# Two subtractions of an attention pipeline, on GpSimd instead of VectorE

## The chip, the cores and the metric

One core of a Trainium2 chip runs the whole kernel in one launch. The metric is the device time of that launch in microseconds. TensorE does the matrix products, VectorE and ScalarE the work on what TensorE leaves in PSUM, GpSimd reads and writes SBUF alone, and SyncE issues most DMAs.

## What is computed

A decoder block over x (8 sequences of 256 tokens, width 512): self attention, cross attention to a context of 256 tokens of width 128, and a mixture of 32 experts. Cut to what matters here:

```python
# self attention of layernorm(x): 16 heads of 32, 4 key heads
cw = sigmoid(sum(abs(x), -1, keepdims=True))
q = dot(x * cw, Wq);  k, v = split(dot(x, Wkv), 2, -1)
qk = einsum('bhid,bhjd->bhij', q, k) * scale + alibi
qk = where(allowed, -1e9, qk);  attn = softmax(qk);  x1 = x + dot(attn @ v, Wo) + bo
# cross attention of layernorm(x1): 32 heads of 16, 8 key heads, k = v = ctx
scores = einsum('bkgsd,bktd->bkgst', qh, kh) / scale
x2 = x1 + softmax(scores) @ vh
# 32 experts, 4 for each token, capacity 128, and a shared one
out = x2 + moe(layernorm(x2)) + shared(layernorm(x2))
```

## The kernel before

The program is one block for each engine, written out in order by hand; engines meet at semaphores. The attention part is a pipeline: `pipelined` calls each engine's body for k = 0 to 9, which the text calls step k. In step k the self attention of sequence k (flag a, k = 0 to 7), the cross attention of sequence k - 1 (flag x, k = 1 to 8) and the routing of sequence k - 2 (flag g, k = 2 to 9) are interleaved. The expert part comes behind and is not touched.

Softmax takes its row maxima ahead of the exponentials. TensorE makes 32 units of cross scores (L1143, two matmuls each, into two halves of qx in turn), and VectorE takes each unit's maximum (L868); TensorE may write unit v only when maximum v - 2 is done. Between these units stand other things, at unit numbers fixed by constants such as `AT_QUERY`, `AT_CONTEXT` and `AT_SELF`: the projection of the queries (L1088), the transposes of values and context (L1097, L1104), of the third norm (L1025), the logits of the router (L1073), and from unit 23 the self scores (L1116, L1118), whose maxima are L859. Then TensorE transposes the maxima (L1168, L1186), and the second half of the step does the scores again with the exponentials and the weighting.

Scores are made exactly enough by splitting. The queries qf (128 x 768, f32, L839 on VectorE) are rounded by ScalarE to qh, and the remainder ql = qf - qh is what L845 computes on VectorE, right behind the maximum of unit 4 (AT_QUERY[3] + 3). It signals q_split. SyncE waits for that and copies qh, qh and ql into the rows of qs by three DMAs of 384 KB; the self scores wait for qs_in. The context keys (128 x 256) are split in three: kp[0] by ScalarE from PSUM, the remainder kr by VectorE (L849), kp[1] by ScalarE, and kp[2] = kr - kp[1] by VectorE (L853), which signals c_split. SyncE then copies them into kxs, which the next step uses. Behind the queries' DMAs SyncE has, in this order: the third norm to xnd, the sequence to out, the wait for c_split and the six DMAs into kxs, then the shift rows of the maxima.

GpSimd's part of step k is: add the bias bo to the two tiles of the sequence (L467), then the powers and products of the norms (L435, L441) as their statistics come, and with flag g the list of slots (L482) and eight indirect DMAs that scatter into slot_table (L487). The last norm of step k and its scatters end during the first units of step k + 1, so in steps 3 to 7 the bias additions stand behind eight scatters. The lines of the order and the signals:

```python
                    hold(sp, s["q_split"], k + 1)
                    for m, part in enumerate((qh, qh, ql)):
                        go(qs[m:SPLIT_ROWS:3].bitcast(F32), part.bitcast(F32), "qs_in")
```

In step 0 there are no cross units, and VectorE does L839, L845, L849 and L853 in a row.

Of the kernel before, what the change touches and what calls it, by code (L numbers as in the profile page):

```python
# [6 lines left out]
F32 = mybir.dt.float32  # L7
# [3 lines left out]
ALU = mybir.AluOpType  # L11
# [97 lines left out]
def build(nc, x, ctx, wq, wkv, wo, bo, gw, gb, w1, w2, w3, sg, su, sd,  # L109
# [15 lines left out]
    with st:  # L125
# [54 lines left out]
        qf = place(DC * SQ).rearrange("p (c n) -> p c n", c=DC)  # L180
        qh = place(DC * SQ, dt=F32R).rearrange("p (c n) -> p c n", c=DC)
        ql = place(DC * SQ, dt=F32R).rearrange("p (c n) -> p c n", c=DC)
# [4 lines left out]
        kr = place(S)  # L187
        kp = [place(S // 2, dt=BF16) for _ in range(3)]
# [82 lines left out]
        s = {n: sem(n) for n in names}  # L271
# [38 lines left out]
        AT_QUERY = (-1, -1, -1, 1)  # L310
# [119 lines left out]
        @block.gpsimd  # L430
        def _(pool):
            def norm_scale(n, count):

                pool.wait_ge(s[f"ln{n}_stats"], count)
                nc.gpsimd.tensor_tensor(stats[n][2][:], stats[n][1][:, :, 1], power[:], ALU.pow  # L435
                                        ).then_inc(s[f"ln{n}_rstd"], 1)

            def norm_shift(n, count):

                hold(pool, s[f"ln{n}_rstd"], count)  # L440
                nc.gpsimd.tensor_tensor(shift[n][:], shift[n][:], stats[n][2][:], ALU.mult  # L441
                                        ).then_inc(s[f"ln{n}_shift"], 1)

            nc.gpsimd.memset(ones[:], 1.0)
            nc.gpsimd.memset(onesb[:], 1.0)
            nc.gpsimd.memset(seen[:], 0.0)
            nc.gpsimd.memset(vx, 1.0)

            nc.gpsimd.memset(arena[:, attention_top:ARENA], 0.0).then_inc(s["clear"], 1)
            for n, (place_, value) in enumerate(((qxs[96:P], 0.0), (kxs[0][96:P], 0.0), (kxs[0][96:98], 1.0),  # L450
                                                 (kxs[1][96:P], 0.0), (kxs[1][96:98], 1.0))):
                pool.wait_ge(s["clear"], n + 1)
                nc.gpsimd.memset(place_, value).then_inc(s["clear"], 1)
            pool.wait_ge(s["clear"], 6)
            pool.wait_ge(s["const_moved"], 1)
            nc.gpsimd.memset(power[:], -0.5).then_inc(s["const_ready"], 1)
            pool.wait_ge(s["const_ready"], 1)
            norm_scale(1, 1)
            norm_shift(1, 1)

            @pipelined(pool)
            def _(k, a, x, g, n):
                if a:

                    pool.wait_ge(s["xn1"], k + 1)
                    for t in range(2):
                        op = nc.gpsimd.tensor_tensor(tile(k, t), tile(k, t), bo_s[:], ALU.add)  # L467
                    op.then_inc(s["bo_added"], 1)
                if n:
                    norm_scale(1, k + 2)  # L470
                    norm_shift(1, k + 2)
                if a:
                    norm_scale(2, k + 1)
                if x:
                    norm_scale(3, k)
                    norm_shift(3, k)
                if g:

                    pool.wait_ge(s["slot_ready"], k - 1)
                    if isinstance(k, int) and k == 2:  # L480
                        pool.wait_ge(s["init_out"], 16)
                    nc.gpsimd.tensor_copy(sdat[:, :, 0].rearrange("p (t k) -> p t k", t=2),  # L482
                                          token[:, bass.ds(k * 2 - 4, 2)].unsqueeze(2).broadcast_to([P, 2, TOPK])
                                          ).then_inc(s["sdat_ready"], 1)
                    hold(pool, s["sdat_ready"], k - 1)
                    for c in range(2 * TOPK):
                        nc.gpsimd.indirect_dma_start(  # L487
                            slot_table, bass.IndirectOffsetOnAxis(ap=slot_u[:, c:c + 1], axis=0), sdat[:, c, :], None,
                            bounds_check=NE * CAP - 1, oob_is_err=False).then_inc(s["sc_out"], 16)

            pool.wait_ge(s["sc_out"], B * 2 * TOPK * 16)
            pool.wait_ge(s["xnd_out"], B * 16)

            pool.wait_ge(s["ks_in"], B * 96)
            pool.wait_ge(s["x2"], B * 3)
            pool.wait_ge(s["slot_ready"], B)
            pool.dma_start(iw[:].rearrange("p (e c) -> p e c", c=2), slot_table.rearrange("(e p) c -> p e c", p=CAP)
                           ).then_inc(s["iw_in"], 16)
            pool.wait_ge(s["iw_in"], 16)

            ids = iw[:].rearrange("p (e c) -> p e c", c=2)

            def fetch(e):

                if e >= FETCH:
                    pool.wait_ge(s["xe_t"], e - FETCH + 1)
                nc.gpsimd.indirect_dma_start(
                    fetched[e % FETCH], None, xnd, bass.IndirectOffsetOnAxis(ap=ids[:, e, 0:1], axis=0),
                    bounds_check=N - 1, oob_is_err=False).then_inc(fetch_in[e % FETCH], 16)

            def add_base(n):

                pool.wait_ge(s["res_final"], n * 4 + 4)
                pool.dma_start(out.rearrange("b (u p) d -> p (b u) d", p=P)[:, n * 4:n * 4 + 4],
                               res[:, n * 4 * D:n * 4 * D + 4 * D].rearrange("p (t d) -> p t d", t=4),
                               accum_op=ALU.add).then_inc(y_out, 16)

            for e in range(FETCH):
                fetch(e)
            pool.wait_ge(s["x2_out"], B * 16)  # L520
            flat = out.rearrange("b s d -> (b s) d")
            for e in range(NE):
                if FETCH <= e + FETCH - 1 < NE and e > 0:
                    fetch(e + FETCH - 1)
                pool.wait_ge(s["y_ready"], e + 1)
                if e > 0:
                    pool.wait_ge(y_out, adds_before(e) * 16)
                nc.gpsimd.indirect_dma_start(  # L528
                    flat, bass.IndirectOffsetOnAxis(ap=ids[:, e, 0:1], axis=0), ye[e % 2], None,
                    bounds_check=N - 1, oob_is_err=False, compute_op=ALU.add).then_inc(y_out, 16)  # L530
                if base_after(e) is not None:
                    pool.wait_ge(y_out, adds_before(e) * 16 + 16)
                    add_base(base_after(e))
            pool.wait_ge(y_out, adds_before(NE) * 16)
# [176 lines left out]
        def _(dve):  # L711
# [116 lines left out]
            def _(k, a, x, g, n):  # L828
# [11 lines left out]
                                     cwb[:, GLOB:S].unsqueeze(1).broadcast_to([P, DC, SQ]), ALU.mult  # L840
                                     ).then_inc(s["q_scaled"], 1)

                def queries_low():
                    dve.wait_ge(s["q_hi"], k + 1)
                    v_.tensor_tensor(ql, qf, qh.bitcast(F32), ALU.subtract).then_inc(s["q_split"], 1)  # L845

                def context_rem():
                    dve.wait_ge(s["c_hi"], k + 1)
                    v_.tensor_tensor(kr, va[:, 0:S], kp[0], ALU.subtract).then_inc(s["c_rem"], 1)  # L849

                def context_low():
                    dve.wait_ge(s["c_mid"], k + 1)
                    v_.tensor_tensor(kp[2], kr, kp[1], ALU.subtract).then_inc(s["c_split"], 1)  # L853

                def self_max(u):

# [5 lines left out]
                if x:  # L862

                    for v in range(XU):
                        kv, t, half = v // 4, v // 2 % 2, v % 2
                        dve.wait_ge(s["xs_unit"], k * XU - XU + v + 1)
                        col = t * XH + query_at(kv * 4 + half * 2)
                        v_.reduce_max(mxx[:, col:col + 3:2], xbank[v % 2].rearrange("p (h n) -> p h n", h=2), AX.X  # L868
                                      ).then_inc(s["x_max"], 1)
                        if a:  # L870
                            if v == AT_QUERY[3] + 1:
                                queries()
                            elif v == AT_QUERY[3] + 3:
                                queries_low()
                            elif v == AT_CONTEXT + 3:
                                context_rem()
                            elif v == AT_CONTEXT + 6:
                                context_low()
                            if v in AT_SELF:
                                self_max(AT_SELF.index(v))  # L880
                    if not a:
# [6 lines left out]
                else:  # L888
                    if a:
                        queries()  # L890
                        queries_low()
                        context_rem()
                        context_low()
                if a:
                    for u in range(len(AT_SELF) if x else 0, AU):
                        self_max(u)
# [542 lines left out]
```

## Time and profile before

| what | value |
|---|---|
| median of 3 runs | 1155.16 us (1154.0 to 1156.06) |
| the profiled execution | 1159.79 us |
| its span | 1158.0 us |
| busy: TensorE, VectorE, ScalarE, GpSimd | 1004.4, 583.8, 332.2, 214.3 us |
| mean granted clock of TensorE | 0.877 |
| steps 1 to 7 | some 82 to 88 us each, between 102 and 707 us |

The profile is one execution. Busy times are shares of different stages, so they don't tell by themselves what ends last; the chain of waits does, since it is followed back from the last instruction. The granted clock is TensorE's, 1.00 for 2.4 GHz and 0.50 for 1.2 GHz. A DMA's time to landing runs from its issue to its signal.

### The profile page before, as it was taken

The numbers are of one execution on the slowest core, as the hardware profiler recorded it, in microseconds if no ns is written. First come the engines' busy times: TensorE is split into PE (matmuls) and PEld (weight loads), VectorE is DVE, ScalarE is ACT, GpSimd is POOL, SyncE is SP. The second block draws the span as 40 slices with busy tenths as digits, with TensorE's granted clock in tenths as the row PEclk, the third lists the DMA queues.
The fourth block names the chain that finished last, engine by engine and source line by source line (L and its number), as shares of the span: only waits on it lengthen the run. The fifth ranks groups of instructions, "written<-read, shape, count | busy, mean of one in ns | idle before, by whom it ended". The sixth has DMA issues, their size and how long they took to land.

```text
span 1158.0 us, 15121 instructions
## 1 busy us (share of the span) xinstructions
PE 1004.4 (87%) x5745; PEld 532.4 (46%) x5784; DVE 583.8 (50%) x1296; ACT 332.2 (29%) x639; POOL 214.3 (19%) x212
## 2 busy tenths in 40 slices
PE   2666898998998998998999798897999999999983
PEld 1535445545545545545535444233444444444441
DVE  1335836857857857857866947723122222222221
ACT  3021064154154154154164143161111111111110
POOL 6001001002102102102102203004322232322222
PEclk9678589689689689689589999698999999999997
DMA  6402202302302302302302404008277776777782
GB/s 214 133 2 73 56 2 74 92 2 74 92 3 74 92 3 73 92 3 73 92 3 74 129 2 128 2 1 291 47 182 211 210 208 215 221 185 218 209 231 33
DMA packets 95579, 119.26 MB, mean 103 GB/s; under 512 B 11185, under 2 KB 72049, under 8 KB 95504
## 3 DMA queue, kind: packets, MB, share of 16 engines
q1 hardware_dynamic: 80644, 96.52, 26.7%
q0 software_dynamic: 11408, 18.64, 8.2%
q10 hardware_dynamic: 3456, 3.15, 0.9%
q8 instruction: 46, 0.75, 0.3%
q14 instruction: 25, 0.20, 0.1%
HBM read 70.90 MB, written 21.07 MB: 79 GB/s over the span
## 4 chain that ended last, share of the span: by engine, by line
PE 71%; DVE 14%; DMA 4%; ACT 4%; issue 3%; POOL 2%; SPq 0%; ACTq 0%; POOLq 0%; DVEq 0%
PE qa L1393 9%; PE qx L1143 5%; PE qa L1257 5%; PE pt L1362 5%; DVE mxx L868 5%; PE qx L1381 4%; PE vb L1210 4%; ACT arena L540 4%; PE qa L1088 4%; PE vb L1037 4%; PE qx L1037 4%; PE qx L1199 3%; PE qa L1118 3%; PE qa L1037 3%; PE va L1057 3%
## 5 line engine op out<-in xcount | busy, mean ns | idle before, releaser
L540 ACT ACTIVATE arena<-qx 128x512 f32<-128x512 f32 x268 | 151.2, 597 | 309.7 <-PE qx L1199 187.4
L868 DVE TENSOR_REDUCE mxx<-qx 128x2 f32<-128x512 f32 x256 | 166.3, 684 | 45.1 <-PE qx L1143 42.8
L1143 PE MATMUL qx<-arena 96*128 96x256 bf16 x512 | 120.6, 344 | 31.4 <-DVE mxx L868 30.9
L435 POOL TENSOR_TENSOR rstd<-mv,power 128x2 f32<-128x2 f32 x24 | 16.9, 702 | 651.6 <-DVE mv L732 651.6
L540 ACT ACTIVATE arena<-qa 128x512 f32<-128x512 f32 (+2 forms) x116 | 63.9, 553 | 217.3 <-PE qa L1393 95.6
L1393 PE MATMUL qa<-arena 128*128 128x512 f32 x256 | 115.2, 593 | 0.8 <-ACT arena L540 0.8
L1199 PE MATMUL qx<-arena 98*128 98x512 bf16 x256 | 98.9, 428 | 8.4 <-ACT arena L540 5.6
L528 POOL DMA_INDIRECT out<-arena,iw x32 | 50.4, 1576 | 209.4 <-DVE arena L997 137.0
L1210 PE MATMUL vb<-arena 128*32 128x256 f32 x1024 | 87.6, 416 | 1.8 <-ACT arena L540 1.1
L1143 PEld LDWEIGHTS qx<-arena 96*128 96x128 bf16 x512 | 41.5, 113 | 91.7 <-DVE mxx L868 74.6
L1118 PE MATMUL qa<-ks,qs 100*128 100x128 f32 x256 | 76.3, 451 | 7.7 <-DMA qs<-arena 7.7
L916 DVE RECIPROCAL rd<-va 128x192 f32<-128x192 f32 x32 | 43.4, 1358 | 58.1 <-PE va L1252 58.1
L487 POOL DMA_INDIRECT slot_table<-sdat,slot_u x64 | 65.8, 1028 | 23.5 <-issue 17.1
L1118 PEld LDWEIGHTS qa<-ks,qs 100*128 100x128 f32 x256 | 65.2, 312 | 7.5
L1393 PEld LDWEIGHTS qa<-arena 128*128 128x128 f32 x256 | 46.5, 192 | 46.9 <-issue 46.9
L1257 PE MATMUL qa<-arena 128*128 128x512 f32 x128 | 60.6, 619 | 5.9 <-DVE arena L918 5.9
L1381 PE MATMUL qx<-arena 128*128 128x512 f32 x128 | 62.0, 608 | 2.3 <-DVE arena L997 2.3
L1362 PE MATMUL pt<-arena 128*128 128x512 f32 x128 | 59.5, 609 | 4.8 <-DVE res L989 2.6
L1006 DVE SCALAR_TENSOR_TENSOR arena<-arena,qa 128x256 f32<-128x256 f32 x32 | 13.5, 421 | 91.8 <-ACT arena L540 91.8
L1199 PEld LDWEIGHTS qx<-arena 98*128 98x128 bf16 x256 | 24.0, 101 | 76.8 <-ACT arena L540 45.9
L859 DVE TENSOR_REDUCE mx<-qa 128x4 f32<-128x512 f32 x64 | 44.0, 689 | 23.1 <-PE qa L1118 22.2
L540 ACT ACTIVATE arena<-arena 128x512 f32<-128x512 f32 (+3 forms) x40 | 25.5, 637 | 84.6 <-DVE arena L839 53.1
(172 smaller groups left out, 1425.6 us busy)
## 6 DMA issues: line engine op xcount, KB each, us to landing
arena<-in_L_ffn_w SPq DMA_DIRECT2D x96, 512.0 KB, 6.0
qs<-arena SPq DMA_DIRECT2D x24, 384.0 KB, 5.0
arena<-arena SPq DMA_DIRECT2D x72, 128.0 KB, 2.4
res<-in_x SPq DMA_DIRECT2D x8, 512.0 KB, 9.0
xnd<-arena SPq DMA_DIRECT2D x8, 512.0 KB, 7.0
out<-res SPq DMA_DIRECT2D x8, 512.0 KB, 7.3
out<-res POOLq DMA_DIRECT2D x4, 1024.0 KB, 9.3
ks<-arena SPq DMA_DIRECT2D x48, 64.0 KB, 1.9
```

The source lines that it names most:

```text
L487: nc.gpsimd.indirect_dma_start(slot_table, bass.IndirectOffsetOnAxis(ap=slot_u[:, c:c + 1], axis=0), sdat[:, c, :], None, bounds_check=NE ...
L540: nc.scalar.activation(dst, src, func, **kw).then_inc(s[signal], 1)
L868: v_.reduce_max(mxx[:, col:col + 3:2], xbank[v % 2].rearrange("p (h n) -> p h n", h=2), AX.X).then_inc(s["x_max"], 1)
L1037: op = mm(bank, w[:, c, m * P:m * P + P], xt3[:, bass.ds(n * 2, 2), c, :], start=c == 0, stop=c == DC - 1)
L1118: op = mm(abank[u % 2][:, h * P:h * P + P], qs[0:rows, q * 4 + h, blk * GLOB:blk * GLOB + P], ks[0:rows, blk, q, :], start=False, stop=h == 3)
L1143: op = mm(xbank[v % 2][:, h * S:h * S + S], qxs[0:XSPLIT_ROWS, query_at(kv * 4 + half * 2 + h), t * P:t * P + P], kxs[1 - k % 2][0:XSPLIT_ ...
L1199: mm(xbank[v % 2], kxs[1 - k % 2][0:XSPLIT_ROWS + SHIFT_ROWS, kv, t * P:t * P + P], qxs[0:XSPLIT_ROWS + SHIFT_ROWS, h:h + 3:2, :], start=T ...
L1210: op = mm(vb[at_:at_ + 32, kv % 2 * S:kv % 2 * S + S], vx[:, t, kv, :], ex[(2 * w + g4 // 2) % 4][:, g4 % 2 * S:g4 % 2 * S + S], start=t = ...
L1257: op = mm(qa[:, t * D:t * D + D], at[:, q, t * P:t * P + P], wo_s[:, q, :], start=q == 0, stop=q == DC - 1)
L1362: op = mm(pt[:, D:2 * D], ht_sh[:, c, m * P:m * P + P], sd_s[:, c, :], start=c == 0, stop=c == DC - 1)
L1381: op = mm(xbank[0], hte[e % 2][:, c, :], h2[e % EU][:, c, :], start=c == 0, stop=c == 1)
L1393: op = mm(abank[e % 2], xgt[e % 2][:, c, :], h13[e % EU][:, c, :], start=c == 0, stop=c == DC - 1)
```

## The change

The subtractions L845 and L853 are taken out of VectorE's order and put into GpSimd's, behind the bias additions of the same step and ahead of the norms. Each waits there for the same signal of ScalarE (q_hi, c_mid) and gives the same signal (q_split, c_split). Operands, sizes and everything else stay.

```diff
@@ gpsimd, step k
                     for t in range(2):
                         op = nc.gpsimd.tensor_tensor(tile(k, t), tile(k, t), bo_s[:], ALU.add)
                     op.then_inc(s["bo_added"], 1)
+                    pool.wait_ge(s["q_hi"], k + 1)
+                    nc.gpsimd.tensor_tensor(ql, qf, qh.bitcast(F32), ALU.subtract).then_inc(s["q_split"], 1)
+                    pool.wait_ge(s["c_mid"], k + 1)
+                    nc.gpsimd.tensor_tensor(kp[2], kr, kp[1], ALU.subtract).then_inc(s["c_split"], 1)
                 if n:
@@ vector, step k
-                def queries_low():
-                    dve.wait_ge(s["q_hi"], k + 1)
-                    v_.tensor_tensor(ql, qf, qh.bitcast(F32), ALU.subtract).then_inc(s["q_split"], 1)
-
...
-                def context_low():
-                    dve.wait_ge(s["c_mid"], k + 1)
-                    v_.tensor_tensor(kp[2], kr, kp[1], ALU.subtract).then_inc(s["c_split"], 1)
...
                             if v == AT_QUERY[3] + 1:
                                 queries()
-                            elif v == AT_QUERY[3] + 3:
-                                queries_low()
                             elif v == AT_CONTEXT + 3:
                                 context_rem()
-                            elif v == AT_CONTEXT + 6:
-                                context_low()
```

GpSimd around the end of one of the steps 2 to 5 and the start of the next, before (the slot list, the scatters of the old step, then the bias additions and norms of the new one):

```order
L482 COPY sdat<-token 128x8
L487 DMA slot_table<-sdat,slot_u 4096x2 x8
L467 TENSOR_TENSOR res<-res,bo_s 128x512 x2
L435 TENSOR_TENSOR rstd<-mv,power 128x2
L441 TENSOR_TENSOR shift<-shift,rstd 128x2
L435 TENSOR_TENSOR rstd<-mv,power 128x2 x2
```

The same place after:

```order
L486 COPY sdat<-token 128x8
L491 DMA slot_table<-sdat,slot_u 4096x2 x8
L467 TENSOR_TENSOR res<-res,bo_s 128x512 x2
L470 TENSOR_TENSOR arena<-arena 128x768
L472 TENSOR_TENSOR arena<-arena 128x256
L435 TENSOR_TENSOR rstd<-mv,power 128x2
L441 TENSOR_TENSOR shift<-shift,rstd 128x2
```

The 768 and 256 columns (ql and kp[2]) now stand behind eight scatters and two additions. VectorE from the start of a middle step to the first self maximum (L859), before; mxx are the cross maxima, mx the self maxima:

```order
L834 TENSOR_TENSOR arena<-va,arena 128x256
L868 TENSOR_REDUCE mxx<-qx 128x2 x3
L839 TENSOR_TENSOR arena<-qa,arena 128x768
L868 TENSOR_REDUCE mxx<-qx 128x2 x2
L845 TENSOR_TENSOR arena<-arena 128x768
L868 TENSOR_REDUCE mxx<-qx 128x2 x6
L849 TENSOR_TENSOR arena<-va,arena 128x256
L868 TENSOR_REDUCE mxx<-qx 128x2 x3
L853 TENSOR_TENSOR arena<-arena 128x256
L868 TENSOR_REDUCE mxx<-qx 128x2 x10
L859 TENSOR_REDUCE mx<-qa 128x4
```

And after, where L864 are the cross maxima, L843 the queries, L849 the remainder kr and L855 the self maxima:

```order
L838 TENSOR_TENSOR arena<-va,arena 128x256
L864 TENSOR_REDUCE mxx<-qx 128x2 x3
L843 TENSOR_TENSOR arena<-qa,arena 128x768
L864 TENSOR_REDUCE mxx<-qx 128x2 x8
L849 TENSOR_TENSOR arena<-va,arena 128x256
L864 TENSOR_REDUCE mxx<-qx 128x2 x13
L855 TENSOR_REDUCE mx<-qa 128x4
```

Two instructions are gone from between the maxima; the rest keeps its order.

## Rows read from the trace of the kernel before

**Rows 1.** The page, part 4: shares of the chain by engine.
```profile
PE 71%; DVE 14%; DMA 4%; ACT 4%; issue 3%; POOL 2%; SPq 0%; ACTq 0%; POOLq 0%; DVEq 0%
```

**Rows 2.** VectorE's groups by form: count, busy us, mean ns, idle before.
```profile
L845 DVE TENSOR_TENSOR arena<-arena 128x768 fp32r<-128x768 f32 x8 | 7.7, 957 | 0.9 <-ACT arena L540 0.9
...
L853 DVE TENSOR_TENSOR arena<-arena 128x256 bf16<-128x256 f32 x8 | 3.3, 416 | 0.5 <-ACT arena L540 0.5
```

**Rows 3.** The chain in step 0: start us, us, what.
```profile
38.06 0.97 DVE arena L845
...
46.60 1.30 PE qa L1118 x4
```

**Rows 4.** The chain in step 1.
```profile
115.58 0.87 DVE arena L845
...
122.55 0.33 DVE arena L853
```

**Rows 5.** The chain in step 2, at the context transposes.
```profile
203.41 0.36 PE va L1104 x2
```

**Rows 6.** ScalarE's timeline in step 2, the copy of the values: start us, us.
```profile
202.50 0.47 ACT L540 ACTIVATE arena<-va 128x384 f32<-128x384 f32 x1
```

**Rows 7.** GpSimd's timeline in steps 3 to 7: scatters and bias additions.
```profile
287.84 1.48 POOL L487 DMA_INDIRECT slot_table<-sdat,slot_u  x1 [0.31 <-issue]
...
291.89 2.50 POOL L467 TENSOR_TENSOR res<-res,bo_s 128x512 f32<-128x512 f32 x2
...
375.14 0.97 POOL L487 DMA_INDIRECT slot_table<-sdat,slot_u  x1 [0.30 <-issue]
...
378.68 2.50 POOL L467 TENSOR_TENSOR res<-res,bo_s 128x512 f32<-128x512 f32 x2
...
461.52 1.74 POOL L487 DMA_INDIRECT slot_table<-sdat,slot_u  x1 [0.30 <-issue]
...
465.83 2.51 POOL L467 TENSOR_TENSOR res<-res,bo_s 128x512 f32<-128x512 f32 x2
...
553.59 2.50 POOL L467 TENSOR_TENSOR res<-res,bo_s 128x512 f32<-128x512 f32 x2
...
641.23 2.50 POOL L467 TENSOR_TENSOR res<-res,bo_s 128x512 f32<-128x512 f32 x2
```

**Rows 8.** VectorE's timeline in steps 4 and 5.
```profile
375.12 1.02 DVE L845 TENSOR_TENSOR arena<-arena 128x768 fp32r<-128x768 f32 x1
...
461.47 0.95 DVE L845 TENSOR_TENSOR arena<-arena 128x768 fp32r<-128x768 f32 x1
```

**Rows 9.** The three DMAs into qs of step 5.
```profile
DMA to landing us min/median/max: 3.7/5.1/6.1
```

**Rows 10.** TensorE's timeline, steps 3 to 7: first self scores, transpose of cross maxima.
```profile
302.24 1.20 PE L1118 MATMUL qa<-ks,qs 100*128 100x128 f32 x4
...
390.08 0.75 PE L1118 MATMUL qa<-ks,qs 100*128 100x128 f32 x4
...
476.17 1.07 PE L1118 MATMUL qa<-ks,qs 100*128 100x128 f32 x4
...
486.45 0.63 PE L1168 MATMUL vb<-ident,mxx 128*32 128x128 f32 x2
...
565.85 1.31 PE L1118 MATMUL qa<-ks,qs 100*128 100x128 f32 x4
...
651.12 0.75 PE L1118 MATMUL qa<-ks,qs 100*128 100x128 f32 x4
...
659.82 0.40 PE L1168 MATMUL vb<-ident,mxx 128*32 128x128 f32 x2 [1.01 <-DVE mxx L868]
```

**Rows 11.** Stretches: busy us (count) of five engines, granted clock, DMA share, GB/s.
```profile
460.00:463.00 3.00, 1.05 (x7) 0.26 (x5) 3.00 (x6) 2.61 (x4) 2.45 (x2) 0.96 0.02 1
...
477.00:487.00 10.00, 10.00 (x47) 8.45 (x46) 8.59 (x15) 0.00 (x0) 0.00 (x0) 0.50 0.00 0
...
652.00:660.00 8.00, 6.01 (x42) 4.38 (x42) 8.00 (x14) 0.00 (x0) 0.00 (x0) 1.00 0.00 0
```

More of the change, by code:

```diff
@@ L890, in _ @@
                         queries()
-                        queries_low()
                         context_rem()
-                        context_low()
                 if a:
```

## The prediction

> **What bounds the kernel now.** I read the page's chain of waits first: TensorE holds 71% of it and VectorE 14%, so an instruction taken from VectorE pays only where VectorE is the chain [rows 1]. The edit lies in the attention pipeline, steps k = 0 to 7, so next I read the chain inside single steps. Step 0 has no cross maxima to hide anything: the remainder of the queries (L845, from 38.06 us, 0.97 us long) releases three DMAs into qs, and TensorE's first self score L1118 starts at 46.60, held by them [rows 3]. The reader should see one fixed delay there, from the end of the remainder to that matmul: 46.60 - 39.03 = 7.57 us. In steps 1 to 7 VectorE interleaves the cross maxima with the four small operations, and L845 is on the chain in all seven, as in step 1 with 0.87 us [rows 4]. The low part of the context keys (L853) is on it in step 1 alone, for 0.33 us [rows 4]; later TensorE's transposes and logits end last around it.
>
> Then I read GpSimd's timeline, since it gets the work. In steps 3 to 7 it is late: it still issues the eight scatters of the step before, and ends its two bias additions only at 294.39, 381.18, 468.34, 556.09 and 643.73 us [rows 7]. VectorE's L845 of steps 4 and 5 begins at 375.12 and 461.47 [rows 8], 6 to 7 us before that.
>
> **What leaves VectorE.** Eight L845 of 0.957 us and eight L853 of 0.416 us [rows 2]. In step 1 both are on the chain: 0.87 + 0.33 = 1.20 us gained [rows 4]. In step 2, without L845 TensorE would reach the context transposes (L1104) some 0.87 us before 203.41 [rows 5], but they wait for ScalarE's copy of the values, which ends at 202.50 + 0.47 = 202.97 [rows 6] and does not hang on L845. So 203.41 - 203.01 = 0.40 us is gained, and L853 gives nothing. Steps 3 to 7 have the same sequence, so 0.4 us is what each could gain if nothing else comes late.
>
> **What GpSimd pays.** The trace has no GpSimd subtraction of 768 columns. The nearest row is its two-input addition of 512 columns, a pair of which takes 2.50 us [rows 7], 1.25 each; 768 / 512 x 1.25 = 1.88 us, which I take. Bounds: VectorE's own 0.95 us [rows 2] below, and two passes, 3.76 us, above, since the output is fp32r, which no GpSimd row here has. The 256-column operation is 0.63 us by the same row; behind it stand only norm_scale and norm_shift, which wait for statistics that VectorE makes only in the softmax stage, so it costs nothing. What SyncE has queued behind q_split and c_split (xnd, out, kxs) moves back by up to 8 us and is read a step later; it is covered as long as the six issues for kxs are through before the shift rows are wanted at the end of the maxima.
>
> The Trainium skill (GPSIMD Engine Reference, 3.1) gives GpSimd about 2.6 cycles per element for such an operation, by which I estimate 768 x 2.6 / 1.2 GHz = 1.66 us; the sum below would then be about 1.1 us smaller.
>
> **The scatters get faster.** In step 5 one scatter takes 1.74 us and not 0.97; it starts at 461.52, with VectorE's L845 (461.47 to 462.42) [rows 7, 8]. Steps 6 and 7 show 1.75 at the same place, step 3 shows 1.48, and step 4 shows 0.97 although L845 begins 0.02 us before that scatter [rows 7, 8]. With L845 gone from VectorE I take these away: GpSimd is done 0.51 us earlier in step 3, 0.77 in step 5, 0.78 in steps 6 and 7. The Trainium skill (SBUF: State Buffer, "SBUF: two separate sides") says that a VectorE operation with two SBUF inputs and GpSimd exclude each other from a shared port pair; three of the five steps agree fully, step 4 does not. By that page the maxima, which read PSUM, stay free of the new GpSimd work too.
>
> **Where the queries land now.** The three DMAs behave alike in every step, those of step 5 with 3.7, 5.1 and 6.1 us from issue to landing [rows 9]. So the self scores can start at the end of the bias additions, less the scatter's gain, plus 1.88 + 7.57 = 9.45 us. Against the first L1118 of now, which is held by the maxima [rows 10]:
> step 3: 293.88 + 9.45 = 303.33 against 302.24, +1.09;
> step 4: 381.18 + 9.45 = 390.63 against 390.08, +0.55;
> step 5: 467.57 + 9.45 = 477.02 against 476.17, +0.85;
> step 6: 555.31 + 9.45 = 564.76 against 565.85, hidden, so the 0.40 of VectorE is gained;
> step 7: 642.95 + 9.45 = 652.40 against 651.12, +1.28.
> Together +3.37 us. What VectorE saves ahead of that point in steps 3, 4, 5 and 7 is not gained: TensorE only waits longer. GpSimd's own start does not move against the step, as it hangs on the third norm of the step before. Step 0: GpSimd has done its additions long before, the remainder takes 1.88 for 0.95, all of it on the chain, +0.93. Steps 1 and 2: GpSimd has issued no scatters and is free before the queries are ready; the data has slack (by step 5's rows 462.42 + 7.57 = 469.99 against a start at 476.17 [rows 8, 10]), so -1.20 and -0.40. Sum: 3.37 + 0.93 - 1.60 = +2.7 us.
>
> **The clock.** In the self scores of step 5 the granted clock was 0.50, in those of step 7 it was 1.00 [rows 11]; from the first L1118 to the transpose L1168 this was 486.45 - 476.17 = 10.28 us and 659.82 - 651.12 = 8.70 us [rows 10]. At 460 to 463 us TensorE was busy 1.05 of 3 us, and its clock began to fall within them, to a mean of 0.96 [rows 11]. In step 7 a wait of some 2 us is put just ahead of the self scores, where none was, so I let it lose the higher level (2.4 GHz) there: 10.28 - 8.70 = +1.58. Whether it does is about even, and any step can win or lose as much when its stalls move.
>
> **Forecast.** +2.7 + 1.58 = +4.3 us. The profiled execution took 1159.79 us with a span of 1158.0, 4.6 above the median of 1155.16; the sum is of differences inside that execution, and I add it to the median: 1159.5 us.
>
> **Rivals.**
> (A) Forecast, 1157.5 to 1162: chance 0.48.
> (B) Faster: the landing is hidden everywhere. Mechanism: the subtraction at VectorE's own 0.95 us, or scatters that shorten in step 4 as well, bring qs in before TensorE asks, so VectorE's saving counts. It decides once the data is there 1.5 to 2 us sooner than worked out (1.28 of step 7 plus the 0.4 saved). Price: -1.20 - 6 x 0.40 = -3.6, step 0 between 0 and +0.93, so about 1152.3. For it: four waits of only 0.6 to 1.3 us against the old start. Against it: the 0.95 bound alone does not do it in steps 3 and 7. Chance 0.09.
> (C) Nothing to measure: the step 7 clock stays, and the wait is half a microsecond shorter in steps 3 to 5 and 7: 2.7 - 2.0 = +0.7, about 1156. Chance 0.22.
> (D) The clock goes against more steps: two of steps 3 to 6 lose another 1.58 each by a later rise, 1162.7. Against: their self scores are already at 0.50 in large part. Chance 0.13.
> (E) GpSimd's fp32r output doubles the subtraction: 1.88 us more in steps 0, 3, 4, 5 and 7, and step 6 turns from -0.40 to +0.80: 9.4 + 1.2 = +10.6 more, 1170. No row speaks for it; on VectorE fp32r output costs 0.957 us, under three times the 0.416 of a third of the columns [rows 2]. Chance 0.08.
>
> A change that doesn't do what it says is left out: GpSimd's order shows the two operations behind the bias additions in every step.
>
> **Numbers.** The likeliest is (A), 1159.5. The range takes in (A), (C), (D) and the half of (B) that step 0 spoils, and leaves (E) out: 1153.5 to 1165. A measurement here can tell about 0.2%, 2.3 us. Slower by more, above 1157.5: (A) nearly whole, (D), (E), 0.66. Within: (C) and edges of (A) and (B), 0.25. Faster, below 1152.9: 0.09.
>
> **What would show it.** In the profile after: L470 of GpSimd near 1.9 us; it starts where the bias additions end in steps 3 to 7; no scatter of 1.75 us; idle time of TensorE ahead of L1118 put down to the DMA into qs in steps 3, 4, 5 and 7 (1 to 2.5 us each) and not in 1, 2 and 6; about 8.5 us of it in step 0; the clock at 0.50 in the self scores of step 7. Without those waits the forecast is wrong, and (B) or (C) holds; an L470 near 3.8 us means (E).

## The result, and the profile after

The changed kernel took 1162.79 us (median of 4 executions, 1162.59 to 1163.26), the kernel before 1155.05 us beside it: 7.7 us more, a ratio of 1.0068 with a 95% interval of 1.0050 to 1.0085. The forecast was 1159.5 us, 4.3 us more. The two profiled executions are only 1162.62 - 1159.79 = 2.8 us apart, because executions of the kernel before spread more than that (1151.4 to 1160.6 us on one chip in the next comparison), and its profiled one is at the slow end. So the profiles serve to compare places, and the ratios to compare kernels. The ratios leave out slow executions, more than 1.5% above the fastest of their kernel (one each of x8 and x11 below).

The page after, parts 1 and 4 (busy us by engine; shares of the chain), against [rows 1]:

```profile
PE 1010.0 (87%) x5784; PEld 539.2 (46%) x5784; DVE 575.4 (50%) x1280; ACT 332.0 (29%) x639; POOL 230.5 (20%) x228
...
PE 64%; DVE 12%; DMA 7%; POOL 6%; issue 6%; ACT 4%; SPq 1%; POOLq 0%; ACTq 0%; DVEq 0%
```

GpSimd's share of the chain went from 2% to 6% and that of DMAs from 4% to 7%. Where they entered is seen in step 3, whose chain (start us, us, what) now runs through GpSimd's queue:

```profile
289.44 0.97 POOL slot_table L491
290.42 0.30 issue
290.72 0.97 POOL slot_table L491
291.69 2.52 POOL res L467 x2
294.21 1.76 POOL arena L470
295.97 0.02 issue
295.99 0.55 SPq L334
...
297.23 6.07 DMA qs<-arena
303.30 0.14 issue
303.43 0.59 PE qa L1106
304.02 0.75 PE qa L1108 x4
```

Scatters, bias additions, subtraction, SyncE, the third DMA, then TensorE: no maximum is on this chain. The first self scores by step, from TensorE's timeline, answer to [rows 10]; the bracket is TensorE's idle time and what ended it:

```profile
303.43 0.59 PE L1106 MATMUL qa<-masks,identb 128*128 128x512 bf16 x1 [1.08 <-DMA qs<-arena]
...
391.53 0.58 PE L1106 MATMUL qa<-masks,identb 128*128 128x512 bf16 x1 [0.94 <-DMA qs<-arena]
...
477.98 0.38 PE L1106 MATMUL qa<-masks,identb 128*128 128x512 bf16 x1 [0.77 <-DMA qs<-arena]
...
565.17 0.53 PE L1106 MATMUL qa<-masks,identb 128*128 128x512 bf16 x1 [0.53 <-DMA qs<-arena]
...
654.22 0.63 PE L1106 MATMUL qa<-masks,identb 128*128 128x512 bf16 x1
```

Steps 3 to 6 wait for the queries, step 7 does not: of the signs that the prediction named, the waits came in steps 3, 4 and 5 (0.8 to 1.1 us), and in step 6 in place of step 7. Here GpSimd's groups by form, after (count, busy us, mean ns), for what VectorE did in [rows 2]:

```profile
L470 POOL TENSOR_TENSOR arena<-arena 128x768 fp32r<-128x768 f32 x8 | 14.5, 1808 | 43.0 <-ACT arena L544 43.0
L472 POOL TENSOR_TENSOR arena<-arena 128x256 bf16<-128x256 f32 x8 | 5.4, 669 | 8.0 <-ACT arena L544 8.0
```

### The profile page after: what moved, and what is told of

It is laid out like the page before. It is cut to its first block, busy times and chain, and to the rows that moved or that the text cites. A ratio compares the mean times of both kernels' runs of the same rounds, so it can differ in the third digit from the quotient of the medians.

```text
span 1160.8 us, 15160 instructions
## 1 busy us (share of the span) xinstructions
PE 1010.0 (87%) x5784; PEld 539.2 (46%) x5784; DVE 575.4 (50%) x1280; ACT 332.0 (29%) x639; POOL 230.5 (20%) x228
## 4 chain that ended last, share of the span: by engine, by line
PE 64%; DVE 12%; DMA 7%; POOL 6%; issue 6%; ACT 4%; SPq 1%; POOLq 0%; ACTq 0%; DVEq 0%
PE qa L1383 8%; PE qa L1247 5%; PE pt L1352 5%; PE qx L1133 4%; PE vb L1200 4%; PE qx L1371 4%; PE vb L1027 4%; PE qx L1027 4%; PE qx L1189 3%; ACT arena L544 3%; PE qa L1108 3%; PE qa L1027 3%; DMA qs<-arena 3%; DMA out<-arena,iw 2%; DVE mxx L864 2%
## 5 line engine op out<-in xcount | busy, mean ns | idle before, releaser
L864 DVE TENSOR_REDUCE mxx<-qx 128x2 f32<-128x512 f32 x256 | 165.6, 685 | 49.0 <-PE qx L1133 47.0
L1133 PEld LDWEIGHTS qx<-arena 96*128 96x128 bf16 x512 | 44.2, 116 | 81.1 <-DVE mxx L864 63.5
L1108 PE MATMUL qa<-ks,qs 100*128 100x128 f32 x256 | 80.6, 471 | 0.0
L1108 PEld LDWEIGHTS qa<-ks,qs 100*128 100x128 f32 x256 | 68.9, 328 | 8.2
L491 POOL DMA_INDIRECT slot_table<-sdat,slot_u x64 | 62.9, 982 | 23.5 <-issue 17.1
L1247 PE MATMUL qa<-arena 128*128 128x512 f32 x128 | 60.6, 619 | 5.9 <-DVE arena L908 5.9
L1352 PE MATMUL pt<-arena 128*128 128x512 f32 x128 | 57.8, 594 | 4.8 <-DVE res L979 2.6
L855 DVE TENSOR_REDUCE mx<-qa 128x4 f32<-128x512 f32 x64 | 44.3, 692 | 31.3 <-PE qa L1108 30.2
L1106 PE MATMUL qa<-masks,identb 128*128 128x512 bf16 x64 | 39.8, 622 | 11.9 <-DMA qs<-arena 11.9
```

What stands on the lines that cost most here:

```text
L491: nc.gpsimd.indirect_dma_start(slot_table, bass.IndirectOffsetOnAxis(ap=slot_u[:, c:c + 1], axis=0), sdat[:, c, :], None, bounds_check=NE ...
L1108: op = mm(abank[u % 2][:, h * P:h * P + P], qs[0:rows, q * 4 + h, blk * GLOB:blk * GLOB + P], ks[0:rows, blk, q, :], start=False, stop=h == 3)
L1133: op = mm(xbank[v % 2][:, h * S:h * S + S], qxs[0:XSPLIT_ROWS, query_at(kv * 4 + half * 2 + h), t * P:t * P + P], kxs[1 - k % 2][0:XSPLIT_ ...
L1247: op = mm(qa[:, t * D:t * D + D], at[:, q, t * P:t * P + P], wo_s[:, q, :], start=q == 0, stop=q == DC - 1)
L1352: op = mm(pt[:, D:2 * D], ht_sh[:, c, m * P:m * P + P], sd_s[:, c, :], start=c == 0, stop=c == DC - 1)
```

## The experiments

All numbers of steps are from the first key matmul of the step to the first self score, in the profiled execution of each kernel. The ratio is to executions of the kernel before on the same chip; chips and hours differ (its median was 1155.05, 1156.66, 1157.04 and 1161.54 us). It is not the quotient of the two medians, from which it differs by up to 0.2%. The columns of steps come from one execution each, and its time is not the median: x10's profiled one took 1155.37 us where its median is 1163.66, x9's 1161.54 for 1169.49.

| kernel | ratio [95%] | step 0 | steps 1, 2 | steps 3 to 7 | steps 0 to 7 | the rest of the span |
|---|---|---|---|---|---|---|
| before | 1 | 21.16 | 26.60, 26.98 | 26.90 27.15 26.88 28.81 26.44 | 210.9 | 947.1 |
| x1 before again | 0.9985 [0.9966, 1.0004] | 21.26 | 26.56, 27.34 | 26.89 28.80 26.44 26.89 27.11 | 211.3 | 946.7 |
| after | 1.0068 [1.0050, 1.0085] | 22.10 | 27.43, 26.59 | 27.79 27.88 27.47 27.47 28.38 | 215.1 | 945.7 |
| x5 after again | 1.0100 [1.0079, 1.0121] | 22.55 | 25.40, 26.62 | 27.75 27.92 27.48 28.38 29.25 | 215.4 | 949.9 |
| x2 delay only | 1.0089 [1.0059, 1.0119] | 23.18 | 28.28, 28.83 | 28.28 27.97 27.46 27.70 27.51 | 219.2 | 945.5 |
| x9 queries only | 1.0070 [1.0041, 1.0100] | 21.44 | 27.48, 26.54 | 27.75 28.02 27.48 27.48 27.52 | 213.7 | 946.0 |
| x10 keys only | 1.0017 [0.9992, 1.0042] | 21.01 | 26.34, 27.43 | 26.89 26.89 26.90 28.90 26.44 | 210.8 | 942.8 |
| x7 before, scatters late | 0.9993 [0.9979, 1.0008] | 21.69 | 28.56, 27.10 | 26.44 26.89 27.11 26.95 26.89 | 211.6 | 946.6 |
| x3 no subtraction | 0.9987 [0.9963, 1.0010] | 20.85 | 27.38, 26.54 | 26.54 28.37 29.23 26.08 26.66 | 211.7 | 943.6 |
| x11 between the additions | 0.9969 [0.9942, 0.9997] | 21.91 | 25.56, 26.54 | 26.64 26.54 26.72 28.41 28.39 | 210.7 | 943.0 |
| x6 ahead of the additions | 0.9927 [0.9903, 0.9951] | 21.88 | 25.95, 26.55 | 26.55 26.74 29.26 26.09 26.55 | 209.6 | 940.4 |
| x4 scatters late | 0.9917 [0.9889, 0.9945] | 21.99 | 27.41, 26.59 | 26.54 26.63 26.76 26.77 26.54 | 209.2 | 942.0 |
| x8 x4, step 0 on VectorE | 0.9946 [0.9926, 0.9967] | 20.49 | 27.48, 26.60 | 26.55 26.65 26.54 26.73 26.54 | 207.6 | 938.7 |
| x12 x6, step 0 on VectorE | 0.9914 [0.9882, 0.9946] | 20.49 | 26.04, 26.58 | 26.54 26.65 29.16 26.09 26.68 | 208.2 | 940.8 |

**x1, the kernel before again.** No edit.

> The kernel before, unchanged. The change cost 7.7 us between medians (1155.05 to 1162.79) but only 2.8 us between the two profiled executions (1159.79 to 1162.62), so the profiled execution of before was 4.7 us over its own median. If that was one odd execution, with the clock's levels falling elsewhere, this profile comes out near 1155 us and its steps 1 to 7 are shorter than those of the first one. If a profile always costs this kernel some 4.7 us, it is near 1159.8 again. The median should be 1155 us, ratio 1.000, either way.

1156.35 us (1151.43 to 1159.78), and again a profile of 1159.78 us. Whether a profiled execution of this kernel always costs more is left open by it: x7's (1159.98) was also the highest of its ten, x10's the lowest of its eleven. The equal total is chance in part: step 7 took 27.11 and not 26.44 us up to the self scores, step 4 28.80 and not 27.15. What differs is where the clock stands. Stretches of x1 in the self scores of steps 5 and 7 (us, busy by engine, then the granted clock), against [rows 11]:

```profile
478.00:486.00 8.00, 6.14 (x43) 4.33 (x42) 8.00 (x15) 0.00 (x0) 0.00 (x0) 1.00 0.01 2
649.00:657.00 8.00, 8.00 (x37) 6.78 (x37) 6.95 (x11) 0.00 (x0) 0.00 (x0) 0.50 0.00 0
```

In the first profile step 7 had the clock at 1.00 there and step 5 at 0.50; in x1 it is the other way round. So neither is a property of a step. In the profiles of before, x1, x3, x6, x7, x8, x10, x11 and x12, one or two steps of each had their self scores at 1.00 (8.70 us to L1168, where 0.50 takes 10.5); in those of the changed kernel (after, x5), x2 and x9, which have the late landing, and of x4, none had. That 1.8 us and the 2 us that a step now and then loses ahead of the self scores (28.4 to 29.3 in the table) wander from execution to execution.

**x2, the delay alone.** VectorE keeps both subtractions; GpSimd repeats the queries' one, and its signal counts.

```diff
-  v_.tensor_tensor(ql, qf, qh.bitcast(F32), ALU.subtract).then_inc(s["q_split"], 1)
+  v_.tensor_tensor(ql, qf, qh.bitcast(F32), ALU.subtract).then_inc(s["q_dve"], 1)
...
   op.then_inc(s["bo_added"], 1)
+  pool.wait_ge(s["q_dve"], k + 1)
+  nc.gpsimd.tensor_tensor(ql, qf, qh.bitcast(F32), ALU.subtract).then_inc(s["q_split"], 1)
```

> VectorE keeps both subtractions, as before; GpSimd does the subtraction of the queries once more behind the bias additions, and only its signal releases SyncE. So the late landing stands alone, without any relief of VectorE. Late landing as the cause: q_split in steps 3 to 7 as late as after the change plus up to 0.8 us for the lengthened scatter, waits of TensorE for qs of 0.5 to 2.5 us, step 0 later by 1.9 us; 1155 + 6 to 9, 1161 to 1165 us. Rival, that the change's loss lies in how the clock falls once VectorE has less to do: the landing costs only what the sum had, some 4 us, about 1159 us.

1167.67 us, ratio 1.0089: with the delay and no relief the whole loss is there; that it is more than the change's 1.0068 can't be told, since the intervals overlap. The waits of TensorE for qs, in x2 and then in the changed kernel (us in total, times, longest):

```profile
PE qa L1120 <- DMA qs<-arena: 12.7, 6, 9.6
```
```profile
PE qa L1106 <- DMA qs<-arena: 11.9, 5, 8.6
```

The longest is step 0, so x2 has 3.1 us in five steps and the changed kernel 3.3 in four. The delay is not quite alone in x2: in steps 0 and 3 the keys' subtraction, still on VectorE, meets GpSimd's and takes 0.93 and 1.20 us in place of 0.42. VectorE's row and GpSimd's in step 3:

```profile
300.04 1.20 DVE L855 TENSOR_TENSOR arena<-arena 128x256 bf16<-128x256 f32 x1
```
```profile
299.14 1.81 POOL L470 TENSOR_TENSOR arena<-arena 128x768 fp32r<-128x768 f32 x1
```

With the queries' subtraction still on VectorE too, GpSimd's timeline of x2 shows the long scatter of step 3 again:

```profile
292.62 1.49 POOL L489 DMA_INDIRECT slot_table<-sdat,slot_u  x1 [0.30 <-issue]
294.41 0.97 POOL L489 DMA_INDIRECT slot_table<-sdat,slot_u  x1 [0.30 <-issue]
```

**x3, the relief alone.** No subtraction of the queries at all; the rounded part is copied three times (so that part of the scores is left out).

```diff
-  v_.tensor_tensor(ql, qf, qh.bitcast(F32), ALU.subtract).then_inc(s["q_split"], 1)
...
-  hold(sp, s["q_split"], k + 1)
-  for m, part in enumerate((qh, qh, ql)):
+  hold(sp, s["q_hi"], k + 1)
+  for m, part in enumerate((qh, qh, qh)):
```

> The subtraction of the queries is left out altogether: SyncE waits for the rounding by ScalarE and copies the rounded part three times. So VectorE is relieved and nothing lands later. Theory of the prediction: step 0 gains 0.95, step 1 0.87, steps 2 to 7 0.40 each, 4.2 us together, 1151 us. Rival (the relief of VectorE is itself worth nothing, or costs, because TensorE then runs the same stretch at the lower clock, as step 1 of the changed kernel showed, which lost 0.83 us where 1.20 was expected as gain): 1154 to 1157 us.

1156.52 us, no difference that can be told; the 4.2 us of the prediction's theory (a ratio of 0.9964) lie at the very edge of the interval. The single steps show both halves of that. Where the clock stood alike, steps 2 and 3, 26.54 us stand against 26.98 and 26.90: 0.44 and 0.36 gained, as the prediction had it, and for its reason. The chain of x3 in step 3 goes through ScalarE between queries and transposes:

```profile
284.28 0.96 DVE arena L839
...
286.01 1.50 ACT arena L546 x2
287.51 0.38 ACT arena L540
287.89 0.04 issue
287.94 0.69 PE va L1097 x2
```

In steps 4 and 5 the clock took it back (28.37 and 29.23 us): it was at 0.54 and 0.50 during the router's logits there, and at 1.00 in step 3.

**x4, the scatters late.** The changed kernel, with the eight scatters of a step issued behind the next step's two subtractions. `scatter` is the slot list and the eight DMAs as a function.

```diff
   nc.gpsimd.tensor_tensor(kp[2], kr, kp[1], ALU.subtract).then_inc(s["c_split"], 1)
+  if k >= 3:
+      scatter(k - 1)
...
-  if g:
...
+  if k == B + 1:
+      scatter(k)
```

> The changed kernel, but the eight scatters of a step are issued behind the next step's two subtractions. The subtraction of the queries then starts when the queries are rounded, in every step. If the late landing is the cause, no wait for qs is left in steps 3 to 7, step 0 still pays 0.9 us, and the time falls to that of before or under it: 1155.05 + 0.93 - 1.20 - 6 x 0.40 = 1152.4 us. If the loss comes from GpSimd working beside VectorE or from the clock, it stays at 1159 to 1163 us.

1149.00 us against 1156.66, ratio 0.9917: faster than both kernels, and by some 3 us more than expected (7.7 us under before, for 2.7). Steps 3 to 7 take 26.5 to 26.8 us, with no wait for qs; that of step 0 is the only one left.

**x5, the changed kernel again.** No edit.

> The changed kernel again, beside the next three, for more executions: 1162 to 1164 us, ratio to before 1.005 to 1.007. In its profile the self scores of steps 3 to 7 start 27.4 to 28.4 us behind the step's start, wherever the clock falls, since the landing sets them.

1168.90 us, ratio 1.0100, above the 1.005 to 1.007 expected; the intervals of the two measurements just touch (the first ends at 1.0085, this one begins at 1.0079). Steps 6 and 7 took 28.38 and 29.25 us up to the self scores, longer than the landing asks for.

**x6, the subtraction ahead of the bias additions.**

```diff
+  pool.wait_ge(s["q_hi"], k + 1)
+  nc.gpsimd.tensor_tensor(ql, qf, qh.bitcast(F32), ALU.subtract).then_inc(s["q_split"], 1)
   pool.wait_ge(s["xn1"], k + 1)
   for t in range(2):
       op = nc.gpsimd.tensor_tensor(tile(k, t), tile(k, t), bo_s[:], ALU.add)
   op.then_inc(s["bo_added"], 1)
-  pool.wait_ge(s["q_hi"], k + 1)
-  nc.gpsimd.tensor_tensor(ql, qf, qh.bitcast(F32), ALU.subtract).then_inc(s["q_split"], 1)
```

> The changed kernel with GpSimd's order turned: scatters, subtraction of the queries, bias additions, subtraction of the keys. The landing comes 2.5 us earlier in steps 3 to 7 than in the changed kernel, some 24.9 to 25.3 us behind the step's start, ahead of the 26.6 that the late scatters gave. If the late landing is the cause: no wait for qs in steps 3 to 7, and the time of the kernel with late scatters, 1149 to 1151 us. If what helped there was moving the scatters, it stays near 1156 to 1160 us.

1148.82 us against 1157.04, ratio 0.9927, as x4. Two instructions of one engine change places, by 2.5 us, and the sign of the whole edit turns. GpSimd's timeline in step 3 and the chain of the same step:

```profile
287.79 1.84 POOL L466 TENSOR_TENSOR arena<-arena 128x768 fp32r<-128x768 f32 x1
289.55 2.52 POOL L469 TENSOR_TENSOR res<-res,bo_s 128x512 f32<-128x512 f32 x2
```
```profile
295.54 2.50 DVE mxx L864 x4
298.03 0.05 issue
298.08 0.39 PE qx L1133 x2
298.47 1.06 PE qa L1108 x4
```

The maxima release the self scores again, 298.47 us here, while the subtraction's end plus 7.57 us gives 289.63 + 7.57 = 297.20.

**x7, the scatters late in the kernel before.** Both subtractions stay on VectorE; GpSimd waits for c_mid ahead of the scatters of the step before.

```diff
   op.then_inc(s["bo_added"], 1)
+  pool.wait_ge(s["c_mid"], k + 1)
+  if k >= 3:
+      scatter(k - 1)
```

> The kernel before, both subtractions on VectorE, with the eight scatters issued only behind the next step's c_mid signal, as in the kernel with late scatters. It tells whether that kernel's gain of 7.7 us is VectorE's relief or the scatters' place. Relief: no change, 1155 to 1157 us. Scatters' place: 1149 to 1151 us.

1156.75 us, ratio 0.9993. The scatters' place is worth nothing by itself, so x4's gain comes with the moved subtractions, once they land early.

**x8, step 0 on VectorE with late scatters.** As x4, with the queries' subtraction of step 0 on VectorE.

```diff
+  if k:
       pool.wait_ge(s["q_hi"], k + 1)
       nc.gpsimd.tensor_tensor(ql, qf, qh.bitcast(F32), ALU.subtract).then_inc(s["q_split"], 1)
...
   queries()
+  dve.wait_ge(s["q_hi"], k + 1)
+  v_.tensor_tensor(ql, qf, qh.bitcast(F32), ALU.subtract).then_inc(s["q_split"], 1)
```

> Late scatters as in x4, and in step 0 the subtraction of the queries stays on VectorE, where nothing covers it. Step 0 should give back 0.8 to 0.9 us: 1148.1 us where x4 had 1149.0. Rival, that a start shifted by 0.8 us moves the clock's levels more than that: anything from 1146 to 1151 us.

1151.2 us, ratio 0.9946, where x4 had 0.9917: the 0.9 us is lost in the spread (seven of its executions lie from 1148.1 to 1154.5 us, one at 1170). In the waits, step 0 has its 7.7 us back in place of 8.6.

**x9, the queries alone.** The queries' subtraction moved, the keys' one left on VectorE.

```diff
   op.then_inc(s["bo_added"], 1)
+  pool.wait_ge(s["q_hi"], k + 1)
+  nc.gpsimd.tensor_tensor(ql, qf, qh.bitcast(F32), ALU.subtract).then_inc(s["q_split"], 1)
```

> Of the change, the move of the queries' subtraction alone; VectorE keeps the keys' one. The late landing is all in this part: ratio to before 1.005 to 1.010, 1163 to 1169 us, as the whole change. If the keys' subtraction on GpSimd has a share in the loss (SyncE's later kxs), it is under 1.005.

1169.49 us against 1161.54, ratio 1.0070: the whole loss is in this part. TensorE waited for qs 5.0 us in five steps besides step 0. As in x2, VectorE's keys' subtraction met GpSimd's, in steps 3, 5 and 6, and took 0.47, 0.67 and 0.81 us there in place of 0.42.

**x10, the keys alone.** The keys' subtraction moved, the queries' one left.

```diff
   op.then_inc(s["bo_added"], 1)
+  pool.wait_ge(s["c_mid"], k + 1)
+  nc.gpsimd.tensor_tensor(kp[2], kr, kp[1], ALU.subtract).then_inc(s["c_split"], 1)
```

> The move of the keys' subtraction alone. It was on the chain in step 1 only, for 0.33 us, and nobody waits for kxs before the next step: no difference, ratio 0.998 to 1.001. Rival, that relief of VectorE between the maxima is what the kernels with an early landing gained their 8 us by, and this part has a share: 0.996 or less.

1163.66 us against 1161.54, ratio 1.0017, interval 0.9992 to 1.0042: no difference, and no share of a gain.

**x11, a dose between.** One bias addition, the queries' subtraction, the other addition.

```diff
-  for t in range(2):
-      op = nc.gpsimd.tensor_tensor(tile(k, t), tile(k, t), bo_s[:], ALU.add)
-  op.then_inc(s["bo_added"], 1)
+  nc.gpsimd.tensor_tensor(tile(k, 0), tile(k, 0), bo_s[:], ALU.add)
   pool.wait_ge(s["q_hi"], k + 1)
   nc.gpsimd.tensor_tensor(ql, qf, qh.bitcast(F32), ALU.subtract).then_inc(s["q_split"], 1)
+  nc.gpsimd.tensor_tensor(tile(k, 1), tile(k, 1), bo_s[:], ALU.add).then_inc(s["bo_added"], 1)
```

> A dose between: GpSimd does one bias addition, then the queries' subtraction, then the other. The landing comes 1.25 us earlier than in the changed kernel (27.5 to 27.9 us behind the step's start in steps 3 to 6), so at 26.3 to 26.6, where TensorE asked for it with an early landing (26.6). If the late landing alone makes the loss, this kernel has nearly all of it back: 1149 to 1152 us, waits of at most 0.2 us. If the time goes by the landing in proportion, with no such point, it lies halfway, near 1157 us.

1156.90 us against 1161.54, ratio 0.9969 [0.9942, 0.9997]. TensorE's only wait for qs is that of step 0:

```profile
PE qa L1105 <- DMA qs<-arena: 8.6, 1, 8.6
```

So the waits go at the point that was expected, and steps 3 to 5 take 26.5 to 26.7 us as with an early landing. But the gain is less than half of x6's, where nearly all of it was expected; it is also not the halfway between x6 and the changed kernel, which would be 1.000. Its interval meets that of x6 and not that of the changed kernel. Whether a landing that is just in time costs in some executions, or this is spread, is open.

**x12, step 0 on VectorE with x6's order.** The edit of x8 on x6.

> The kernel with the queries' subtraction ahead of the bias additions (x6, 1148.8 us), with VectorE doing it in step 0. By step 0's 0.93 us: 1147.9 us, ratio to before some 0.992. The kernel with late scatters and the same edit came out at 1151.2, against 1149.0 without it, with executions up to 7 us apart; if the clock's levels drown the 0.9 us again, anything from 1146 to 1152 us.

1149.39 us against 1161.54, ratio 0.9914 [0.9882, 0.9946], the fastest by ratio, though not told apart from x6 and x4. In its profile step 0 reaches the self scores after 20.49 us, x6's after 21.88.

## Why the prediction was right, and where its size was off

**The direction and its cause** held. The chain of step 3, x2 (the delay without the relief, 1.0089), x9 (queries alone, 1.0070), x10 (keys alone, no difference) and x6 (2.5 us earlier, 0.9927) show that the late landing makes the loss.

**GpSimd's subtraction**: 1.88 us taken, 1.81 measured; 0.63 and 0.67 for the keys. Rival (E), fp32r at double cost, is out. The estimate by the Trainium skill (GPSIMD Engine Reference, 3.1), 1.66 us, was lower than the trace, whose bias additions were the better row.

**The scatters**: none in steps 3 to 7 takes over 1.19 us any more, and x2, which keeps the queries' subtraction on VectorE, has a 1.49 again in step 3. The row was read rightly. The exception of step 4 is no property of that step: x1 and x10 have 1.75 there, and x10 has the exception in step 6. VectorE's and GpSimd's rows of x10 in steps 6 and 7:

```profile
545.30 1.02 DVE L847 TENSOR_TENSOR arena<-arena 128x768 fp32r<-128x768 f32 x1
...
633.09 0.95 DVE L847 TENSOR_TENSOR arena<-arena 128x768 fp32r<-128x768 f32 x1
```
```profile
545.33 0.97 POOL L489 DMA_INDIRECT slot_table<-sdat,slot_u  x1 [0.30 <-issue]
...
633.12 1.76 POOL L489 DMA_INDIRECT slot_table<-sdat,slot_u  x1 [0.30 <-issue]
```

A few nanoseconds decide it. In the profiles of before, x1, x2 and x10 the subtraction and a scatter meet 20 times. In the six where the scatter started 19 to 33 ns behind the subtraction, the scatter kept its 0.97 us and the subtraction took 1.01 to 1.02; in the ten with 34 to 52 ns the scatter took 1.74 to 1.76 and the subtraction 0.95; in the four of step 3, with some 0.3 us, the scatter took 1.47 to 1.49.

**The landing**: the end of the subtraction plus 7.57 us. Step 3: 295.96 + 7.57 = 303.53, and the scores' own L1108 started at 303.46, overlapping L1106, which adds the mask; step 0: 39.96 + 7.57 = 47.53, measured 47.53. Step 0 lost 22.10 - 21.16 = 0.94 us for 0.93 forecast. The forecast starts of steps 3 to 5, as differences to before within the step, were +1.09, +0.55, +0.85; measured +0.89, +0.73, +0.59.

**Steps 6 and 7** were wrong as single steps; steps 3 to 7 were nearly right as a sum. Step 6 was to gain 0.40 with no wait; it waited 0.53 us and still gained 28.81 - 27.47 = 1.34 us, since its 28.81 before was the clock's: granted 0.57 during the router's logits, for 0.91 after. Step 7 was to wait; it came 1.94 us later without a wait, because TensorE had the clock at 0.52 in the logits. The stretch of the changed kernel:

```profile
640.00:650.00 10.00, 9.26 (x36) 4.08 (x33) 6.28 (x10) 1.82 (x3) 6.19 (x6) 0.52 0.31 72
```

Steps 3 to 7 together: 138.99 - 136.18 = +2.81 us for the +3.37 of the sum. Over three profiles with the late landing (after, x5, x9) their mean is 139.3, over four of before, x1, x7 and x10 it is 135.7: +3.7.

**Steps 1 and 2**: -1.60 expected, 54.02 - 53.58 = +0.44 found in the first pair. Step 2 gained its 0.39. Step 1 lost 0.83, in two parts. Its keys' projection (L1057, L1047 after) took 102.26 to 106.93 us before and 102.82 to 108.94 after, 1.45 us longer, since the clock rose later there; that wanders too (25.40 us for the step in x5, 28.56 in x7). From there to the self scores it gained 21.93 - 21.31 = 0.62 us, not 1.20. The chain of step 1 after shows why an instruction's time on the chain is not gained in full:

```profile
123.46 0.70 DVE mxx L864
124.16 0.05 issue
124.21 0.62 PE qx L1133 x2
124.83 0.02 issue
124.85 0.70 DVE mxx L864
```

At the lower clock a maximum and the unit that waits for it take 1.39 us for two units, where two maxima back to back take VectorE 1.28 us (before, from 122.80), so part of what is taken from VectorE falls into its idle time. Over the three profiles with the late landing and the four of before, x1, x7 and x10, steps 1 and 2 gained 0.9 us together for the 1.60 forecast.

**The clock** is the term that was mis-sized most. It was put at +1.58 us, all in the self scores of step 7. In the first pair of profiles that came true: from the first self score to the transpose, step 7 took 8.70 us before and 664.81 - 654.29 = 10.52 after.

```profile
664.81 0.63 PE L1158 MATMUL vb<-ident,mxx 128*32 128x128 f32 x2
```

That it was step 7 was luck, since x1 had 10.52 us there without the change and its 8.71 in step 5. Summed over steps 1 to 7, the same stretch took 72.2 to 73.5 us in after, x5 and x9 and 68.9 to 70.8 in before, x1, x7 and x10, in the mean +2.6 us. Up to the self scores, steps 0 to 7 took 214.7 us in the mean of the first three and 211.2 in that of the four: +3.6 us, for the +2.7 of the sum. Together these are 6.1 us in place of 4.3. The change cost 7.7 us between medians, and 11.9 in x5; what lies over 6.1 is not found in the profiles, whose spans are only 5.0 us apart in the mean, and stays open.

So of the rivals' numbers it is (D)'s 1162.7, the clock against more steps, that the 1162.79 us meet, and (A)'s own 1157.5 to 1162 ends just under it; the result is inside the stated range of 1153.5 to 1165. (D)'s mechanism is not in the first pair: the self scores of steps 3 to 6 took 41.05 us before and 41.12 after.

The granted clock is known for every execution, and it goes with the late landing on each chip: in the median 0.870 in x2 where before had 0.8765, 0.863 in x5 for 0.876, 0.863 in x9 for 0.870. The kernels that land early had 0.8825 (x4) for 0.8765, 0.878 (x6) for 0.876 and 0.876 (x12) for 0.870. That the waits themselves keep the clock down is a correlation and not shown; it stays open.

**Rival (B)** gave 1152.3 us for a landing that is always hidden. The kernels that hide it, x4 and x6, came out at 7.7 and 8.2 us under before, not 2.8. The part up to the self scores gained 210.9 - 209.4 = 1.5 us in their profiles, the rest of the span some 6. Some 2 us of that rest lie in one stretch without any of the moved work, from the transposes of the maxima of step 8 to the first down product of the shared expert (L1362): 58.5 us in x3, x4, x6, x8 and x12, and 60.6 to 62.6 in before, after and the others but x2 (57.8). The granted clock differs there, 0.92 and 0.83 before and 0.95 and 0.91 in x6 (us, busy by engine, clock; before, then x6):

```profile
739.60:779.60 40.00, 36.93 (x211) 13.95 (x212) 16.56 (x63) 19.71 (x37) 0.75 (x2) 0.92 0.01 1
779.60:800.20 20.60, 14.74 (x44) 6.62 (x42) 8.71 (x39) 4.22 (x7) 8.17 (x10) 0.83 0.80 273
```
```profile
734.40:774.40 40.00, 36.91 (x213) 14.15 (x214) 16.62 (x63) 19.70 (x37) 1.05 (x3) 0.95 0.01 1
774.40:793.00 18.60, 12.74 (x41) 5.51 (x39) 8.75 (x39) 4.21 (x7) 7.85 (x8) 0.91 0.83 282
```

Neither half of the move shows a gain alone: without the queries' subtraction (x3, 0.9987) and with the keys' one on GpSimd (x10, 1.0017) nothing could be measured, while x4 and x6 have both. So the gain seems to need both subtractions gone from VectorE, but the kernel that would tell, with the queries' one alone ahead of the bias additions, was not run. Why they would act only together is not settled.

## What to carry to other kernels

An instruction given to an idle engine starts when that engine's queue lets it, not when its input is ready: look up what stands ahead of it in the receiving queue at that moment, add the transfer behind it, and compare with the moment its reader asks. Here the same instruction lost 0.7 to 1.0% behind 2.5 us of additions that nobody was waiting for (no wait in the profiles of before and after is put down to them), and gained 0.7% ahead of them. And a clock level seen in one step of one profile is worth nothing as a term of a sum until a second profile of the same kernel shows it there.

## What the runs showed of the hardware

A scatter that GpSimd issues while VectorE does a subtraction with both inputs in SBUF took 1.47 to 1.76 us in place of 0.97, if it started 34 ns or more behind the subtraction; if it started at most 33 ns behind, it kept its 0.97 us and the subtraction took 1.01 to 1.02 us in place of 0.95. With the subtraction gone from VectorE no scatter of steps 3 to 7 took over 1.19 us. The other way round, a 0.42 us subtraction on VectorE with both inputs in SBUF took 0.47 to 1.20 us beside GpSimd's 1.8 us subtraction (x2, x9).

VectorE operations with an input in PSUM were not slowed by GpSimd's subtraction: in the profile after, the 21 cross maxima that ran beside it took 687 ns in the mean, the other 235 took 685; in x6, six of the eight L849 ran beside it and took 413 to 425 ns, where before had 414 to 426 without it. All cross maxima together took 685 ns in the mean, for 684 before:

```profile
L864 DVE TENSOR_REDUCE mxx<-qx 128x2 f32<-128x512 f32 x256 | 165.6, 685 | 49.0 <-PE qx L1133 47.0
```

The kernel before, the same program each time, spread over 1151.4 to 1159.8 us in ten executions on one chip, and its median over chips and hours from 1155.05 to 1161.54; only executions side by side tell kernels apart at this size.
